# Deformable convolution: the coefficient matrix A stored by V tile instead of by product

## The reference, cut to what matters

```python
om = conv3x3(x, w_om) + b_om                       # 27 channels: 9 x (dy, dx), 9 masks
ys = dy + ky + y - 1;  xs = dx + kx + x - 1        # a sampling point for each tap and pixel
vals = bilinear_sample(x, ys, xs) * sigmoid(mask)  # (b, 32, 9, H, W)
out = einsum('bckhw,ock->bohw', vals, weight) + bias
```

## Time and profile before

| | |
|---|---|
| median of 3 runs | 2406.02 us |
| profiled execution | 2404.01 us |
| its span | 2402.0 us |
| PE busy | 2034.2 us (85%), 50241 matmul instructions |
| ACT busy | 1787.6 us (74%) |
| DVE busy | 1585.7 us (66%) |
| POOL busy | 1400.8 us (58%) |
| V matmuls, L971 | 16384 instructions, 816.9 us busy |
| copies pE to A, L731 on DVE | 768, 716.9 us |
| copies pE to A, L565 on ACT | 768, 659.7 us |
| L950 expansion | 24576 instructions, 411.3 us busy |

### The profile page before, as it was taken

How to read it: one execution, slowest core, us unless ns; L and a number is a source line. 1 busy time by engine, 2 the same in 40 slices (tenths; PEclk the granted TensorE clock), 3 DMA queues, 4 the chain that set the end, 5 groups by cost and what they waited for, 6 DMA issues and landing times.

```text
span 2402.0 us, 126528 instructions
## 1 busy us (share of the span) xinstructions
PE 2034.2 (85%) x50241; PEld 1359.9 (57%) x50241; DVE 1585.7 (66%) x2558; ACT 1787.6 (74%) x3238; POOL 1400.8 (58%) x1803
## 2 busy tenths in 40 slices
PE   8555188988988998898998899889889888988985
PEld 3311056666666666666666666666666666666663
DVE  8699066666666666666666666666666666666663
ACT  0003488888888888888888888888888888888884
POOL 0000166666666666666666666666666666666662
PEclk9699599999999999999999999999999999999997
DMA  8036545556555555655555555565555556556553
GB/s 311 1 140 271 200 115 154 147 149 156 143 149 150 147 151 148 156 143 150 152 147 151 151 154 147 148 156 144 148 152 146 150 148 155 145 149 154 145 151 87
DMA packets 196541, 363.81 MB, mean 151 GB/s; under 512 B 39760, under 2 KB 122480, under 8 KB 192368
## 3 DMA queue, kind: packets, MB, share of 16 engines
q1 hardware_dynamic: 196464, 362.74, 55.7%
HBM read 159.38 MB, written 52.22 MB: 88 GB/s over the span
## 4 chain that ended last, share of the span: by engine, by line
PE 29%; ACT 21%; issue 21%; SPq 5%; DVE 5%; POOL 2%; ACTq 1%; DVEq 1%; DMA 0%; POOLq 0%
PE pV L971 8%; PE pM L996 8%; ACT halves L559 7%; ACT big L585 5%; PE pE L950 5%; SPq L405 4%; PE pR L1016 4%; ACT big L576 4%; PE pM L983 4%; ACT big L598 3%; DVE big L731 2%; DVE big L718 1%; ACT msk L589 1%; POOL halves L478 1%; POOL prod L469 1%
## 5 line engine op out<-in xcount | busy, mean ns | idle before, releaser
L478 POOL TENSOR_TENSOR halves<-prod,halves 128x300 f16<-128x300 f32 x768 | 626.4, 816 | 377.2 <-ACT halves L559 377.1
L731 DVE COPY big<-pE 128x768 f32<-128x768 f32 x768 | 716.9, 933 | 191.3 <-PE pE L950 189.0
L971 PE MATMUL pV<-big 128*32 128x144 f32 x16384 | 816.9, 331 | 4.7 <-issue 1.4
L565 ACT ACTIVATE big<-pE 128x768 f32<-128x768 f32 x768 | 659.7, 859 | 107.7 <-PE pE L950 107.6
L469 POOL TENSOR_TENSOR prod<-big 128x300 f32<-128x300 f32 x768 | 554.2, 722 | 100.8 <-POOL big L493 32.2
L718 DVE STREAM_TRANSPOSE big<-halves 128x384 f32<-128x384 f32 x768 | 440.2, 573 | 197.2 <-POOL halves L478 193.4
L950 PE MATMUL pE<-big,sel_s 32*128 32x64 f16 (+1 forms) x24576 | 411.3, 203 | 174.8 <-DVE big L731 103.6
L950 PEld LDWEIGHTS pE<-big,sel_s 32*128 32x128 f16 x24576 | 329.6, 92 | 386.0 <-issue 373.4
L971 PEld LDWEIGHTS pV<-big 128*32 128x32 f32 x16384 | 482.2, 112 | 102.2 <-issue 6.7
L559 ACT ACTIVATE halves<-prod 128x300 f16<-128x300 f32 x768 | 484.3, 631 | 3.2 <-POOL prod L469 3.0
L493 POOL TENSOR_TENSOR big<-big,msk 128x360 f32<-128x360 f32 x128 | 107.2, 838 | 484.5 <-ACT big L579 484.5
(11 more groups left out here) (72 smaller groups left out, 1175.1 us busy)
## 6 DMA issues: line engine op xcount, KB each, us to landing
v<-big SPq DMA_DIRECT2D x1536, 96.0 KB
win<-xh_scratch SPq DMA_DIRECT2D x128, 544.0 KB, 4.2
big<-xh_scratch SPq DMA_DIRECT2D x384, 136.0 KB, 4.1
xh_scratch<-win SPq DMA_DIRECT2D x32, 544.0 KB, 2.7
big<-in_x SPq DMA_DIRECT2D x16, 1024.0 KB, 16.4
x_scratch<-big SPq DMA_DIRECT2D x16, 1024.0 KB, 3.9
x1r<-x_scratch SPq DMA_DIRECT2D x128, 128.0 KB, 2.1
out<-outs SPq DMA_DIRECT2D x128, 128.0 KB, 1.8
```

Source lines behind the costliest of these rows:

```text
L478: nc.gpsimd.tensor_tensor(half[:, rn % 2, :, 0:SQ, 1], prod[:, rn % 2, :, :], half[:, rn % 2, :, 0:SQ, 0], ALU.subtract).then_inc(low_done, 1)
L565: nc.scalar.activation(*expanded(1 - q, r, 0), ACT.Copy).then_inc(e_act, 1)
L731: nc.vector.tensor_copy(*expanded(1 - q, r, 1)).then_inc(e_dve, 1)
L971: last = mm(pV[r % 2][b * C:(b + 1) * C, o:o + TAPC], XT[q][:, t * P + b * C:t * P + (b + 1) * C], av[:, b * NT + t, :, :], start=True, st ...
```

## The change

The address in A becomes n × 144 + round × 24 + u × 6 + kx × 2 + j. The 144 values of a tile now stand side by side, and the V matmul reads them in one piece. The order of the 144 is the same as before, so V and all behind it are untouched. The copies write runs of 6 values (24 bytes), a run every 576 bytes, and read six pE values 64 apart (256 bytes) in turn. kx rises in the products, `perm` follows, and pE's bank is (kx, j, n); the two slots of one ox now adjoin in the source (32 values), and the matmul writes them in runs of 16. Instruction counts, waits and the order on every engine stay.

```diff
--- before.py
+++ after.py
@@ -304,8 +304,8 @@
         def expanded(q, r, h):
 
             src = pE[:, h * 1024:(h + 1) * 1024].rearrange("p (a n) -> p a n", a=2)[:, :, 0:RPX]
-            return A[q][:, r * RW + h * (RW // 2):r * RW + (h + 1) * (RW // 2)] \
-                .rearrange("p (a n j) -> p a n j", a=2, j=2), src.rearrange("p a (j n) -> p a n j", j=2)
+            dst = A[q].rearrange("p (n r a m) -> p r a n m", n=SLOT, r=ROUNDS, a=QUADS)
+            return dst[:, r, 2 * h:2 * h + 2], src.rearrange("p a (m n) -> p a n m", n=SLOT)
 
         def rounds(on, N, q, r, ahead):
 
@@ -932,21 +932,15 @@
                 wait(pe, e_dve, n * ROUNDS + rn)
                 i, ky = rn % TILE_R, rn // TILE_R
                 for ox in range(KS + 1):
-                    slots = [(kx, ox - kx) for kx in range(KS - 1, -1, -1) if 0 <= ox - kx < 2]
+                    slots = [(kx, ox - kx) for kx in range(KS) if 0 <= ox - kx < 2]
+                    at = slots[0][0] * BLK + slots[0][1] * NT
+                    to = (slots[0][0] * 2 + slots[0][1]) * SLOT
                     for h, u in itertools.product(range(2), range(QUADS)):
                         part = slice(u * BLK, (u + 1) * BLK)
                         src = PH[part, rn % 2, :, h].rearrange("p (b m) -> p b m", b=IPG)
-                        dst = pE[:, u * 512:u * 512 + RPX]
-                        at = [(KS - 1 - kx) * BLK + j * NT for kx, j in slots]
-                        to = [j * KS * SLOT + kx * SLOT for kx, j in slots]
-                        if len(slots) == 1:
-                            rhs = src[:, :, at[0]:at[0] + NT]
-                            o = dst[:, to[0]:to[0] + SLOT]
-                        else:
-                            e = to[1] - to[0]
-                            rhs = PH[part, rn % 2, :, h].rearrange("p (b a m) -> p a b m", b=IPG, a=2)
-                            rhs = rhs[:, :, :, at[0]:at[0] + NT]
-                            o = dst[:, to[0]:to[0] + 2 * e].rearrange("p (h n) -> p h n", h=2)[:, :, 0:SLOT]
+                        rhs = src[:, :, at:at + len(slots) * NT].rearrange("p b (a t) -> p b a t", t=NT)
+                        o = pE[:, u * 512 + to:u * 512 + to + len(slots) * SLOT] \
+                            .rearrange("p (a b t) -> p b a t", b=IPG, t=NT)
                         last = mm(o, sel_s[part, (i + ky) * (KS + 1) + ox, :], rhs, start=(h == 0), stop=(h == 1))
                 last.then_inc(e_done, 1)
 
@@ -964,13 +958,13 @@
                         before = r - 2 if r >= 2 else len(VGROUPS) - 2 + r
                         a = V_ACT[before]
                         wait(pe, (v_dve, v_act)[a], (n if r >= 2 else n - 1) * VN[a] + v_count(a, before) + 1)
-                        av = A[q].rearrange("p (m n j) -> p n m j", n=SLOT, j=2)
+                        av = A[q].rearrange("p (n m) -> p n m", n=SLOT)
                         for t in tiles:
                             o = (t - tiles[0]) * TAPC
                             for b in range(IPG):
                                 last = mm(pV[r % 2][b * C:(b + 1) * C, o:o + TAPC],
                                           XT[q][:, t * P + b * C:t * P + (b + 1) * C],
-                                          av[:, b * NT + t, :, :], start=True, stop=True)
+                                          av[:, b * NT + t, :], start=True, stop=True)
                         last.then_inc(v_done, 1)
                     if on[0] and r == OM_AT:
                         wait(pe, sub_done, N)
@@ -1076,7 +1070,7 @@
         for k in range(TAPS):
             ky, kx = divmod(k, KS)
             for b in range(IPG):
-                perm[b * C + f * TAPS + k, f * TAPS * IPG + ky * RB + b * KS + KS - 1 - kx] = 1
+                perm[b * C + f * TAPS + k, f * TAPS * IPG + ky * RB + b * KS + kx] = 1
     a["perm"] = perm
     sel = np.zeros((QUADS, BLK, TILE_R + KS - 1, KS + 1, REG_C // TILE_C, REG_R, TILE_C), np.float16)
     for u in range(QUADS):
```

## The result

The changed kernel takes 2315.65 us (median of 4 runs, 2315.21 to 2317.05), against 2405.02 us before (4 runs). The ratio is 0.9633, interval 0.9614 to 0.9651: 3.7% faster, 89 us. Forecast were 2357 us and a range of 2338 to 2408.

A forecast was written before the change was run, and what follows sets the result against it. A step was bound by a chain of PE 2.9, DVE 2.0, PE 3.0 and ACT 8.2 us. V saved 48 us in the loop and 1.1 behind it, copies and expansion 0: 2357 us, range 2338 to 2408.

The forecast's parts named there:

- The V matmuls: V's reads at L971: adjoining words instead of far pairs cut a quad from 165 to 127 ns, 49 us altogether.
- The path through PE and DVE: Main loop: 10 of V's quads per step (r4, r0) lie on the path, 38 ns each, 48 us; later idle gaps absorb the shift.
- From L569 (1011.91) to there: Main-loop step, from ACT's L569 to the end of r3's copy L565 (1019.99): 8.1 us unaffected by PE's speed.
- The copies: L565 on ACT and L731 on DVE, four on the path: scattered writing changes a step by −0.09 to +0.52 us; taken as 0.
- I take 0: Value chosen for the copies L565 and L731 out of −12 to +66 us, after gapped-write row L664.
- lower end of −23: Best case for one copy L565: 836 ns for 768 elements at L576's rate, against 859.
- Rival 4: More than PE's share: copies L565 and L731 also quicken by 23 ns, 12 us more, 2345 us; chance 0.07.
- Rivals 1 to 3: V's four streams stay slow, 2406 us (0.12); scattered write outweighs gain, 2424 (0.12); half the gain, 2382 (0.07).
- rival 1: V's four streams stay slow in any layout, tiles 9216 bytes apart perhaps hitting the same memory part: 2406 us; chance 0.12.

## Why the prediction was wrong

**The V matmuls.** Right in size: 286 ns against an expected 283 to 290, a quad 128 and 125 ns where 127 stood. The rows of L983 and L1016 had it. The picture behind it, readers that fetch a new place for every second word, is not what the runs show: as many pairs, 504 bytes apart, took 301 ns, and 24 bytes apart 292. And the two matmuls of the earlier trace rows were not quite without neighbours: four others ran until 1321.74, over the start of both (1321.56 and 1321.70). The two started singly and not in fours; more they don't show.

**The path through PE and DVE.** Right: 10 quads a step, 48.7 us measured alone. DVE's and ACT's idle time behind L996 and L983 took the shift, as said.

**"From L569 (1011.91) to there ACT works without a gap of its own: 8.1 us in which PE's speed counts for nothing."** This step failed, twice over, and it is worth 39.9 us.
- There was a wait in it. L598 of r1 waited for the transposes and so for V of r1. Queued operations overlap by a tenth of a microsecond or so (L569 lasts 0.47 us, and L585 starts 0.37 behind its start), so a wait of that length leaves no idle time in the timeline. The start-to-start time of L589 and L598 shows it, 0.22 us on average against 0.11 when PE is early: 0.11 × 127 = 14 us.
- ACT's speed was taken as its own. The rest, (8.11 − 0.11) − 7.80 = 0.20 us by the means of the steps, 25 us, is ACT working undisturbed. It lies in the three parts of the stretch that have V beside them, untouched L579 included, and the kernel that reads adjoining words and writes the old layout shows that V's reading alone does it.

**The copies.** "I take 0" was right for the scattered write (2315.0 against 2315.65), and nearly right for the four copies on the path: the three L565 changed by −11, −8 and +3 ns, and L731 in the mean by +2. But the mean of all L565 fell by 36 ns, below the lower end of −23. That end scaled L576 up to 836 ns, and no floor can be had from it: the L565 in the earlier trace rows, which runs without V beside it, lasts 0.80 us already before the change. A mean over six rounds had hidden that three of them were slow.

**The rivals and the range.** Rival 4, more than PE's share, went the right way with 12 us in place of 40, but named the copies, which brought little on the path; L559, L579, L585 and the earlier L598 were in no term. So nothing in the range could reach below 2338. Rivals 1 to 3 did not happen; rival 1's worry, four streams of equal low address bits, is answered by the kernel in which all four read the same adjoining words: V 291 on average, 2317.06 us.

## What to carry to other kernels

- Before an access pattern is judged by its own engine's path, look for operations of other engines that are slower beside it than elsewhere: their share of the gain doesn't stand in any wait. A mean over all rounds can hide it; take the same operation round by round.
- "Works without a gap" must be checked by start-to-start times of the same pair of operations over many steps. A chain of nearly equal length behind a busy stretch shows no idle time, and it decides what a further cut is worth.
- An experiment that treats only the rounds off the supposed path costs one line and is the direct test of the path.

## What the runs showed of the hardware

- Four fp32 matmuls on 32-column strips with moving reads of pairs at a pitch of 512 bytes: 329 ns for 144 columns; at 504 bytes 301; runs of 4 words at 512 bytes, or all adjoining, 286. At 24 bytes 292, with the four also further apart. Two matmuls with the same pairs at 512 bytes that started singly took 283 and 292; how the time grows with the number of streams was not tried.
- The slow pattern also slowed ACT's work on SBUF (L579 942 → 896 ns without it), and DVE's copy only when the copies had their new pattern (933 → 964).
- The case nobody expected: four streams that read equal addresses at the 512-byte pitch. V 434 ns, DVE's copy 1341, L579 2333 ns, the kernel 31% slower. Equal addresses of adjoining words cost nothing that one run can show (2317.06 us).
- Not settled is what makes 512 bytes bad. A bank chosen by low address bits does not fit the kernel with the four b 8 bytes apart, and no other pitch than 504 and 24 bytes was tried. Nor was it tried whether ACT is held up in reading or in writing, and whether the copies' own 13 ns come from the write or from the read of pE.
